# Moving the loads of x from the SP queue to the ACT queue in the attention steps

## The reference

```
def rmsnorm(t, w): return t * rsqrt(mean(t*t, -1) + 1e-6) * w

def attention(x):                      # layer 0: 32 query heads, 8 key/value groups, D = 128
    q = rope(rmsnorm(x @ Wq.T, q_norm_w), pos)
    k = rope(rmsnorm(x @ Wk.T, k_norm_w), pos)
    v = x @ Wv.T
    kc, vc = k_cache[block_table], v_cache[block_table]     # 16 pages of 32 keys for each sequence
    scores = q @ concat(kc, k).T / sqrt(D), cached keys beyond cache_seqlens masked
    return (softmax(scores) @ concat(vc, v)) @ Wo.T

x = x + attention(x)
x = x + linear_with_lora(x, labels)            # layer 1
x = x + mixture_of_lora_experts(x, languages)  # layer 2
x = x + gated_mlp_with_lora(x, lora_indices)   # layer 3
```

## Time and profile before

| | us |
|---|---|
| three runs | 1406.97, 1406.88, 1404.13 |
| median | 1406.88 |
| profiled execution, device time | 1408.86 |
| its span from first to last instruction | 1407.0 |
| PE busy, share of the span | 1390.5, 99% |
| DVE, ACT, POOL busy | 1095.4, 853.0, 803.2 |
| data moved by DMA | 129.87 MB, mean 92 GB/s |
| granted clock of PE | full in all slices |

### The profile page before, as it was taken

The page is one execution under the profiler, slowest core; times in us unless marked ns, Lnnn a source line. Parts: engine busy times, 40 slices in busy tenths (PEclk is TensorE's granted clock), DMA queues, the critical chain, the costliest instruction groups (busy, mean ns, idle before and its releaser), DMA issues.

```text
span 1407.0 us, 26951 instructions
## 1 busy us (share of the span) xinstructions
PE 1390.5 (99%) x8035; PEld 1204.2 (86%) x8035; DVE 1095.4 (78%) x2220; ACT 853.0 (61%) x2092; POOL 803.2 (57%) x799
## 2 busy tenths in 40 slices
PE   8999999999999999999999999999999999999999
PEld 5788888888888888888888888888888888888887
DVE  7888888888888888888888888888888666654543
ACT  6666666666666666666666666666677423433332
POOL 7555555555555666666666666666566331444442
PEclk9999999999999999999999999999999999999999
DMA  5533333333333222222222222222232550343341
GB/s 189 163 109 109 109 102 102 102 104 101 102 105 107 70 71 77 67 70 65 66 66 66 65 67 72 75 67 51 73 95 63 157 106 24 103 135 113 113 124 68
DMA packets 191440, 129.87 MB, mean 92 GB/s; under 512 B 118832, under 2 KB 158384, under 8 KB 188864
## 3 DMA queue, kind: packets, MB, share of 16 engines
q1 hardware_dynamic: 190592, 126.97, 32.7%
q0 software_dynamic: 416, 1.11, 0.2%
q10 hardware_dynamic: 288, 0.07, 0.0%
HBM read 125.25 MB, written 24.64 MB: 107 GB/s over the span
## 4 chain that ended last, share of the span: by engine, by line
PE 74%; SPq 19%; issue 4%; POOL 1%; DVE 1%; DMA 0%; ACT 0%; POOLq 0%
PE banks L328 18%; PE banks L329 18%; PE banks L330 17%; SPq L348 9%; PE banks L1451 9%; PE banks L1425 7%; SPq L341 5%; SPq L401 4%; PE banks L1387 1%; SPq L375 1%; PE banks L1682 1%; PE banks L1696 1%; PE banks L1509 1%; SPq L372 1%; PE banks L1635 1%
## 5 line engine op out<-in xcount | busy, mean ns | idle before, releaser
L750 ACT ACTIVATE prob<-prob,nbias 128x640 f32<-128x640 f32 x256 | 210.2, 822 | 146.2 <-DVE nbias L1032 146.2
L1003 DVE TENSOR_TENSOR pt_pair<-banks,pt_pair 128x640 fp32r<-128x640 f32 x256 | 210.8, 823 | 102.0 <-ACT pt_pair L746 99.4
L1032 DVE CUSTOM_DVE_ANT_0 prob<-banks,mask,q_rs 128x640 f32<-128x640 f32 x256 | 220.1, 878 | 37.4 <-PE banks L330 37.4
L1451 PE MATMUL banks<-w_pair,o_pair 128*128 128x512 f32 x768 | 223.7, 414 | 0.0
L746 ACT ACTIVATE pt_pair<-banks 128x640 fp32r<-128x640 f32 x256 | 179.3, 700 | 38.7 <-PE banks L1425 38.7
L1425 PE MATMUL banks<-ident,prob 128*128 128x128 f32 x1280 | 184.2, 275 | 1.4 <-DVE pt_pair L1003 1.1
L1425 PEld LDWEIGHTS banks<-ident,prob 128*128 128x128 f32 x1280 | 146.6, 140 | 43.6 <-issue 31.7
L328 PE MATMUL banks<-w_pair,x_pair 128*128 128x256 f32 (+1 forms) x512 | 178.0, 348 | 3.8 <-DVE acc L1057 3.3
L329 PE MATMUL banks<-w_pair,x_pair 128*128 128x256 f32 (+1 forms) x512 | 172.8, 337 | 0.0
L330 PE MATMUL banks<-w_pair,x_pair 128*128 128x256 f32 (+1 forms) x512 | 172.2, 336 | 0.0
L328 PE MATMUL banks<-kt_pair,qt_pair 128*128 128x320 f32 x512 | 163.7, 320 | 0.8 <-DVE kt_pair L1003 0.8
(11 more groups left out here) (196 smaller groups left out, 3434.8 us busy)
## 6 DMA issues: line engine op xcount, KB each, us to landing
w_raw<-in_w_att SPq DMA_DIRECT2D x56, 320.0 KB, 3.2
w_raw<-in_fw SPq DMA_DIRECT2D x66, 256.0 KB, 3.4
x_raw<-in_xT SPq DMA_DIRECT2D x64, 256.0 KB, 3.2
kt_all<-in_kT SPq DMA_DIRECT2D x128, 128.0 KB, 2.5
kv_raw<-in_kv SPq DMA_DIRECT2D x384, 32.0 KB, 1.6
kt_raw<-kt_all SPq DMA_DIRECT2D x38, 256.0 KB, 3.0
kv_raw<-in_kv SPq DMA_DIRECT2D x608, 16.0 KB, 1.5
fb_all<-in_gu_b SPq DMA_DIRECT2D x32, 176.0 KB
```

Source lines behind the costliest of these rows:

```text
L750: act.activation(prob[:, h, :], prob[:, h, :], ACT.Exp, bias=nbias[:, h:h + 1], scale=-1.0, accum_out=psum_row[:, h:h + 1]).then_inc(exped, 1)
L1003: dve.tensor_tensor(pair[1], src, pair[0].bitcast(F32), ALU.subtract).then_inc(lo_sem, 1)
L1032: dve.tensor_tensor_reduce(out=prob[:, h, :].rearrange("p (a n) -> p a n", a=2), in0=score_ps[h % 2][:, :, 0:HALF], in1=mask[:, n % B, :]. ...
L1451: last = pe.matmul(misc_ps, o_pair[:, j, h, :], w_pair[:, k, ds(at + h * HID, HID)], start=i == 0, stop=i == 3 * REP - 1)
```

## The change

The two lines that issued x leave SP's step. ACT issues the same DMA, with the same wait and the same semaphore, in a new function `load_next_x`, which its step calls after `pt_high(n, 2)`. It does so for n = 0 to 60, so 61 of the 64 loads of x move; the first three are issued before the steps and stay on SP.

```
-                if x:
-                    sp.wait_ge(x_lo, n + 2)
-                    load_x(n + 3, 1 - par)
                 load_kv(n + 2, par, True)
...
-                step(n, n % 2, x=n + 3 < NT, w=n < last_w)
+                step(n, n % 2, w=n < last_w)
...
+            def load_next_x(n, par):
+
+                if n + 3 < NT:
+                    act.wait_ge(x_lo, n + 2)
+                    act.dma_start(x_raw[:, 1 - par, :],
+                                  t["xT"][ds((n + 3) % B), :, :].rearrange("a p n -> p (a n)")).then_inc(s_xin[1 - par], 16)
...
                 pt_high(n, 2)
+                load_next_x(n, par)
```

## The result

| us | changed kernel | kernel before, same chip |
|---|---|---|
| median | 1405.23 (22 runs) | 1406.91 (22 runs) |
| lowest to highest | 1402.76 to 1408.16 | 1404.13 to 1409.99 |
| profiled execution: device time, span | 1408.16, 1406.0 | 1408.86, 1407.0 |

The ratio is 0.9985 (95% interval 0.998 to 0.9991). The changed kernel is faster by 1.7 us in the medians, 2.1 by the ratio. That is less than the 4.4 forecast and less than the 0.2% that was set as the bound of a difference. Between its device time and its span lie 2.16 us, where the kernel before had 1.86: in the repeated runs of the two kernels it is 2.12 and 2.13 against 1.80 to 1.83 in the mean. So 0.3 us of what the span gains does not reach the device time; what takes them is not shown.

The account below looks back on a forecast made before the run. It took SP's late page issues, holding up PE before step 26, as the bound. Page waits -5.2, ACT's issue 0 and acc's delay +0.8 gave -4.4 us: 1402.5 us against the median 1406.88, range 1400.5 to 1408.0.

Parts of the forecast that it names:

- SP's step shrinks by 0.47 us and falls below PE's: SP's queue, each step: without x's issue its step goes from 17.28 to 16.81 us, against PE's 17.15.
- All eight waits go, -5.2: PE's weight side before the cached-key transposes, 60 to 500 us: eight waits for pages vanish, -5.2 us (bounds 0 and -5.3).
- What it moves in time: step 2: x(4) is issued by ACT while acc is loading; PE's wait in step 2 becomes about 4.1 us instead of 3.32.
- +0.8 for x(4) beside acc: x(4)'s 262144 bytes share the full DMA engines with acc's load and delay it: +0.8 us (bounds 0 and 0.8).
- ACT's issue costs 0: The 0.4 us issue in each of 61 steps fits ACT's 2.29 us idle time before the exponential: costs 0.
- The first TENSOR_LOAD shorter by up to 0.35: SP's L341 load, 1.60 us median, may shorten by up to 0.35 with one transfer ahead instead of two; not counted.
- SP waits for `v_lo` again in most steps from about 16 on: Sign on SP: it waits for POOL's semaphore that lets it issue pages, 0.2 to 1 us in most steps.
- Nothing gained, 1406: Rival: SP loses about 0.4 us a step on page issues beside ACT's issue or transfer; about 1406 us, chance 0.22.
- Slower, 1420: Rival: x's transfer stalls SP's page issues, 1.0 us a step, bursts of 9.5 us or more; 1420 us, chance 0.13.
- The range: Forecast time of the whole kernel: 1400.5 to 1408.0 us; the likeliest case's own range is 1400.5 to 1404.
- The chance of 0.65: Whole kernel faster by over 0.2% (2.8 us): the forecast case 0.60 and more gained 0.05.

Follow-up runs that it names:

- all four combinations: On one chip, x on SP or ACT, acc in one load or split: 1409.18 and 1407.34 us (SP), 1404.91 and 1403.66 us (ACT).

## Why the prediction was right and where it was wrong

- **SP's step shrinks by 0.47 us and falls below PE's.** Right, and the register loads gave 0.18 more. The slot put back with another transfer, with register loads longer by 0.38, brings the waits back and takes the whole gain.
- **All eight waits go, -5.2.** The waits went, and the 18 steps took 308.71 us, as forecast (308.7). As a term of the sum it was mis-sized, and this is the step that failed. It took the waits of one execution for the price of late paging: a slow one, 2.0 us above the median, with the longest page issues of all fourteen profiles. In the second profile of the kernel before, with page issues 4.6 us shorter in sum and 4.68 us lost in step 2, the waits were 0.5. The three pairs of medians give -1.7, -4.3 and -2.6 (ratios 0.9985, 0.9965, 0.9976), so the forecast -4.4 lies just beyond the largest. Another 0.3 us is a term that the sum did not have: the time outside the span, taken as the same 1.86, grew by it.
- **What it moves in time: step 2.** The prediction saw PE's wait for acc as a fixed 3.32 us plus 0.8. It did not ask which of the two stalls covers the other, nor what PE's clock does after such a wait. Wait and clock are now on the path: step 2 lost 1.75 to 5.86 us in the changed kernel's three profiles, and likely less in an average execution than these three show, as they were the slowest of their runs.
- **+0.8 for x(4) beside acc.** Wrong. The wait was 2.96 us instead of the 4.1 expected, and the first packet of x(4) moved 2.86 us after its issue, when 988 of acc's 1024 had started. acc landed in 8.5 to 10.3 us with x(4) on ACT, in 8.7 to 10.3 with it on SP, in 9.53 without it. The 0.8 was supported by the Trainium skill, "DMA: Bandwidth & Descriptors", Queues, rings and completion order: each DMA engine takes turns between the queues that it has work for. The trace agrees with that from 53.5 us on, when both queues moved about the same (0.17 and 0.16 MB in a microsecond). In the 2.86 us before, ACT's queue got no turn; whether the engines had work from it by then the trace does not tell. The prediction's step from this rule to a sharing of acc's time is what did not hold.
- **ACT's issue costs 0.** Right, and for a stronger reason than given: it began 0.01 us into the copy, was 0.36 us long, and the next exponential still ended an idle time of 2.29.
- **The first TENSOR_LOAD shorter by up to 0.35.** Half of that: 1.595 to 1.411 us. The reason given, one transfer ahead instead of two, is not borne out: with weights and 8 KB ahead it was 1.338.
- **SP waits for `v_lo` again in most steps from about 16 on.** Right, and earlier than forecast: 14 times in 60 to 460 us, seven of them before 300 us, where PE is in step 15.
- **Nothing gained, 1406.** The measured 1405.23 is nearer to this number than to the forecast, but its mechanism is refuted: of the 64 page issues that were under way while ACT issued x, 63 took 315 to 324 ns. By the rule of the Trainium skill ("Perfetto Trace Analysis", on the HWDGE instruction), that the block which makes the descriptors is locked for one issuer at a time, they should have been held up by about 0.36 us; the traces do not bear that out for SP and ACT. The median alone would not show it, as it is one issue in 16, but these issues do.
- **Slower, 1420.** Refuted by the time, and by the bursts of 16 pages: 8.69 us in the median, 8.88 in the kernel before, where 9.5 or more was the sign.
- **The range** held the time. The chance of 0.65 for faster by over 0.2% was given to a gain that came out at 0.15% in this pair and at 0.35% and 0.24% in the two others. A cause for the difference between the pairs is not shown beyond what one profile of each tells: start-up, clock and the length of SP's issues each vary by 2 us and more from execution to execution in either kernel.

## What to carry to other kernels

When one queue is late by a little everywhere, the stalls of the engine that it feeds and that engine's other stalls can cover each other, and the wait that a profile shows is only what is left over: a stall of 4.68 us in step 2 and waits of 5.7 us for pages stood in each other's place. Before pricing a wait, find what else delays the same engine in the stretch in which the queue could catch up. How much that matters in an average execution is a question for the medians of all four combinations, and here they hardly showed it. Take a term of a few microseconds from two profiles of the kernel, not from one: here they showed 5.3 and 0.5 us of the same wait. And look where the profiled execution stands among the runs: the three of the changed kernel were each the slowest.

## What the hardware showed

- ACT issued x (0.33 to 0.39 us) while its ACTIVATE of 0.70 us ran, 61 times, and the ACTIVATE became no longer. SP's page issues beside it took 315 to 324 ns in 63 of 64 cases, as all others do in the median (316).
- With 2048 KB under way on SP's queue, the first packet of a load issued by ACT moved 2.84 to 2.96 us after the issue in five profiles; the median of all loads of x is 1.0.
- The time of an issue on SP did not depend on the bytes: 0.42 us for 256 KB and for 8 KB, both over 128 partitions.
- Of SP's page issues of over 0.9 us before 460 us, 15 of 16 in the first profile of the kernel before and 14 of 14 in the first of the changed kernel fell on the transfer of a 16 KB packet of instruction fetch.
- After PE's wait for acc the clock was at 1.2 GHz in five of nine executions and at 2.4 in four: half after waits of 1.78, 2.56, 2.88, 2.96 and 3.36 us, full after 1.52, 1.73, 1.90 and 3.32. So the length of the wait alone does not decide. Step 2 lost 1.8 to 2.9 us beyond the wait where the clock fell, and about 0.25 where it did not.
- The load of 2048 KB took 8.5 to 10.3 us from issue to landing, for no reason in the program that the runs tell. The start-up of the kernel ended at 27.1 to 29.7 us. Four executions, the second of the kernel before and two of the changed kernel among them, had the half clock for 3.4 us between 15.8 and 19.8, and they are the four latest (29.19 to 29.66); but without it the range is still 27.10 to 29.13.
